# A decoder kernel's step table found anew, with a charge in its planner for changes between bf16 and fp32 operands on TensorE

## The chip, the cores and the metric

One core of one Trainium2 chip runs the whole kernel. The time is device microseconds (us), the median of several runs. The engines are TensorE (PE; its weight loads are PEld), VectorE (DVE), ScalarE (ACT), GpSimd (POOL) and SyncE (SP), which only issues DMAs here.

## The reference, cut to what matters

Twelve sublayers follow each other on `x` of 4 batches x 256 tokens x 128 channels, all fp32:

```python
x = _layernorm(x + _L0_attn_ref(x, ...))         # state-space scan ("mamba")
x = _layernorm(x + _L0_xattn_ref(x, ctx, ctx))   # attention over a context
x = _layernorm(x + _L0_ffn_ref(x, ...))          # attention, then 8 experts, top 2, with a capacity
x = _layernorm(x + _L1_attn_ref(x, weight))      # attention whose values are 128 wide per head
x = _layernorm(x + _L1_xattn_ref(x, ctx, ...))
x = _layernorm(x + _L1_ffn_ref(x, ...))          # 8 experts
x = _layernorm(x + _L2_attn_ref(x, ...))         # causal attention
x = _layernorm(x + _L2_xattn_ref(x, ctx, mask))  # attention with a bias and a mask
x = _layernorm(x + _L2_ffn_ref(x, ...))          # 8 experts, tokens sent to slots
x = _layernorm(x + _L3_attn_ref(x, ...))         # linear attention
x = _layernorm(x + _L3_xattn_ref(x, ctx, ...))   # gathers the nearest context rows, then attention
x = _layernorm(x + _L3_ffn_ref(x, ...))          # 8 experts
```

Attention has 16 heads of 8 channels.

## The kernel before

The work is cut into 2378 steps, each a tuple such as `("P2", a, b, i)`: a kind, a sublayer's number, a batch and an index. A step uses one engine or several in turn: `SM` is scores on TensorE and then their row maximum on VectorE, `P2` is scores again, transposed and shifted by the maximum, on TensorE and then exp on ScalarE, `PV` is the weighted sum of values. `lanes()` puts the steps into 47 queues with a fixed order inside each (one for each batch's chain of sublayers, one for all `SM`, one for all `P2`, and so on). The string `ORDER` says from which queue the next step is taken, one letter for each step. This gives one list of all steps, and each engine's program is this list, cut to the steps that the engine has a part in, with semaphore waits for what a step reads. So `ORDER` alone sets what each engine does after what.

`plan()` goes through the list once, when the program is built, with the durations in `COST` and `cost()`, the time `HOP` that a result takes from one engine to the next, and `needs()`. It decides two more things: which of the eight PSUM banks a TensorE step gets (the bank that comes free first), and where TensorE gets `FILL` steps, matmuls on a free bank that nobody reads. They are put in where the planner sees TensorE idle for over 0.8 us (`FILL_OVER`), for 0.6 of the gap. No time of `plan()` is used on the chip in another way.

What a matmul of each kind looks like matters for the change. The scores of `SM` (L1087) and `P2` (L1116) are bf16 with contraction over 48 or 50 rows, and two heads run side by side in the two halves of the array's rows, on two banks. Before them a causal step has L1082 or L1106 and a masked `P2` has L1111: bf16 over all 128 rows. `MT` (L1096) is bf16 on 16 columns of the array. `MB` and `MC` (L1013) are bf16 over 96 rows. `PV` (L1129) is fp32 on 32 columns, with four heads side by side in the columns. Nearly all else is fp32 over 128 rows and 128 columns: `MA` (L1017), `XT` (L1027), `QK` (L1057), `ZV` (L1139), `Y` (L1155), the experts' `MH` (L1227) and `MO` (L1233). `FILL` (L1001) is bf16 over the whole array.

The times below call a place in the kernel by its line. `held` keeps which step had a bank before, and TensorE waits for the semaphore `read[kind]` of that step, by its count, before it writes there.

Of the kernel before, what the change touches and what calls it, by code (L numbers as in the profile page):

```python
# [54 lines left out]

COST = {
    "DT": ((PE, 1.8), (ACT, 0.7)), "BC": ((PE, 1.2), (DVE, 3.0)), "DZ": ((PE, 0.9), (ACT, 2.0)), "DL": ((ACT, 0.75), (DVE, 1.4)),
    "MX": ((ACT, 0.72),), "MB": ((PE, 0.24), (DVE, 2.34)), "MC": ((PE, 0.22), (ACT, 0.6)), "ME": ((POOL, 1.25),), "MN": ((PE, 0.05),), "MA": ((PE, 0.95),),
    "MY": ((DVE, 0.9), (PE, 0.4)),
    "STAT": ((DVE, 1.2), (POOL, 0.95)), "XB": ((POOL, 0.8),), "STAT2": ((DVE, 1.95), (POOL, 0.95)), "NORM": ((DVE, 0.62),), "XT": ((PE, 0.22), (ACT, 0.33)),  # L60
    "GQ": ((PE, 0.43), (ACT, 0.3)), "GS": ((PE, 0.43), (DVE, 1.7)), "GT": ((PE, 0.44), (ACT, 0.5)), "GM": ((PE, 0.86), (ACT, 0.3)),
# [18 lines left out]
KB = {"RH": 256, "RL": 512, "ROWS": 768, "SHIFT": 8, "GB": 8, "GL": 256, "BL": 192, "YS": 192, "LW": 1024,  # L80
      ("LD", "w"): 2048, ("LD", "part"): 2048, ("LD", "wide"): 1024, ("LD", "mask"): 1536, ("LD", "mask2"): 512, ("LD", "mask3"): 512, ("LD", "lin"): 2048,
      ("LD", "select"): 576, ("LD", "ctx"): 128, ("LD", "zero"): 1920}
HOP = 0.15
PIPE = 0.2
FILL, FILL_OVER, FILL_ONE = 0.6, 0.8, 0.22
TABLE = {"P2": "exp", "LF": "exp", "DZ": "exp", "MX": "exp", "DL": "exp"}
# [127 lines left out]
def needs(st, feats):  # L214
# [248 lines left out]

SYMBOLS = "abcdefghijklmnopqrstuvwxyzABCDEFGHIJKLMNOPQRSTU"
ORDER = (
    "aaaaaaaababaccdebcbaeddacedbcaebaceddbabcebdaceaebcbddacedabcedbacebdcaedbcaebaecbdcaebdcaeddbacedaecebadecdcnbbonacebda"
    "baednecdcaebacbeddonlblacokabocbeedadcedcamblbedaecbadaleccdemmmggggemdepqpmggfphggpglfgfsklhgqhiiggijimhfqmgijmgiqgvihg"
    "ilgggjjnnhlhmgniiknfnniijgghnglmggmmitjghliigggijghghjigioimohiggjugoioiojgoiggmhojiglghghjhgplpiiikggpgjiphpgpijiipukmm"
    "ihgljggjimmqqlghghifqgigqmjqkiiSfggfiqjhgmqiiglgfhsjjmgghivtninilgnggjihnighngimnjgjnighminwggwwwwjinghhngiookggiojiorrr"
    "ggijiiirojxxoghxhxgjowpggpowywyxihxhyiypoikyoiyxxjjipiiyyyyiprjnpnpjpwwwwqqpwwxxrrrxqpynnxxwwyyyrnwqqwlkxxxwxryyrqlrmmmx"  # L470
    "xqwyqxwxywwyyyxqoyqrrrwyyywwoooyyxggxoyggwlwmygkyglhxwgpkxgkhwxxpkkkxwwxpggiyprkyimyijxjpmhxhyllggygykmgggyiyygmyjjjjqjq"
    "gmqkikkkkgiiqgjkjqhgghhlgjkjjmigjjghgRijjijjljnhijmmikjijhjjnijkgggjnkkgilggijjlggmmmjkhjjhggikkkgjjjihgokgikijjohijjjig"
    "ojgjiglmlmgjjRjjgijkjjgpkikkigkpkgmhhhhpgjijjgiggljgjijjkiglhmjimhjjgjjijjijijijiiqggiqjhmgikgqihggljgjhgimlnngigignjhmi"
    "nhhniggjiinmigjgnkinjgiiioonrhggjowgrgowwggxrokgwwhxwhwwigxgojyiyyxxihiyrjyoighixxhxyjyiipjypoyyipjnnniporiirwwwwpjjnwpw"
    "wxxxxprrxqlyqxpmwlykxqyqqypyqrrmxwxywyyyqwqwwrxxyymxwwwooroyxqwxyyyrxxxrwyogwgllgyrryggxyyywtpphwmmgwpwgxxxygygphwlxiyyy"
    "yxlmxigghgyymyhgmqkmiqigjjiqqiTghiglggslijhggggggjmhignmnihggnjninihgiinjnmgilggijglggjkhiihmmhkggojoimivhgoggooijiiuggi"
    "ojghghojlpigpgglkipisippgmpgjjhhiiiiimhpiggjmgjlqqihqggiggTijQgqtlhqmmiqgiggjiiggihqvimjigjlghhnlTkggnghmmiiggnigigjunjn"
    "gggiimgiinRihgjjonhohggghokiogRoiigihjhiggoignjiigiijoojkphhipzBBBpiiijiBiRjippiiCjACDjCwqqqDwwqqEwwFEwwpFDwEwpqFwEpCwRF"
    "GqwEwFwqEwEFDwwFECwwzEDwwGFFwBBBEwFEwwFEwwEwwBGFwFEECCFGFDADCwwGHwCEwwFEwwFEHHHnwwnFGDwEwooEFwnwIIwFEwIIDFEwwIIEIwFwEFJJ"
    "oCDwwJFJGEwwFJEKwwFEwGwJFEwwFwGKKKKKJUEEFFGIIHHLHLLLIJLMLLLIMLLLIHNNNNLNKKNJNLNJOMPRqOOLLLKOPpJJLpLNNNKNKIPLMKLqLNNINNLL"  # L480
    "JMIOOLJOOKILPPNNNNNNnKNJnnpnnnnnJLnILPLMKINnLKOOJJOOLLnKKMLLLnIMPINNNnJNPINNIMlJNOONKLOJKlPlLLLOMPKJlMLlLLoKILoLoMoINoNo"
    "oNJNNJqolUmloKINIooJoLLKkOOONNJoPKLLLIPlOINNNIPKNlMNJlOLOmmNNPgNJKLJOKMOLLLPpLLLlggNlppppINppppNKNNllJINNIpMJgkgOOPNJpLK"
    "OMLOUKKLLpggLLLpLPlgNPNNllNOghNgmmmhNNNgOgROOghlPhPqlgiilglqqqqqqqhqggUiqqmqgijmhgijqimlgiiljljhiikhnnglignlgnilngjjmgnl"
    "hhgniinwmwwgingmgirrjwjghihioiowwoxrxkwgxygjryxiiooyggjgyiiyhoxgowgxyiwgjhggjoiwiwhpyhoxpijipwwxprrjiyiyiipppwxyyxjpjywr"
    "qqxxxxywypqyqqwwwrrqxwqxryyxyyxxxyqywywqrwrrxxxwoowxxnnnrryywwxxoryyywwwyyywpypwpxxyyyyyxxxyyyyqqq"
)


# [5 lines left out]
def plan():  # L494

    queues = lanes()
    feats = [st[1:] for q in queues for st in q if st[0] == "LF"]
    heads = [0] * len(queues)
    free, done, listed = [0.0] * 5, {}, []
    until, place = [0.0] * 8, {}  # L500
    in_table, moved = None, 0.0
    for symbol in ORDER:
        j = SYMBOLS.index(symbol)
        st = queues[j][heads[j]]
        heads[j] += 1
# [24 lines left out]
        if st[0] == "MY" and st[1] % 2:  # L530
            until[place[("MN", st[1] // 2), 0]] = t + HOP
        if st[0] == "LR":
            until[place[("LN", *st[1:]), 0]] = t + HOP
        if st[0] == "STAT" and SUBLAYERS[st[1]] not in (("attn", SELF_WIDE), ("moe", DISPATCHED)):
            until[place[stat_source(st), 0]] = t + HOP
# [29 lines left out]
def decoder(nc, I, scratch, gate_rows_out, lin_out, slots_in, slots_out, out):  # L565
# [12 lines left out]
    with ExitStack() as ctx:  # L578
# [398 lines left out]
        def _(pe):  # L977
# [1170 lines left out]
```

## Time and profile before

| | |
|---|---|
| median of 3 runs | 1210.09 us (1208.85 to 1210.41) |
| profiled execution: its own time | 1201.47 us |
| profiled execution: span, first to last instruction | 1199.6 us |
| mean granted TensorE clock | 0.976 of full |
| TensorE busy | 1106.6 us (92%) |
| VectorE busy | 911.0 us (76%) |
| ScalarE busy | 700.7 us (58%) |
| GpSimd busy | 332.1 us (28%) |
| DMA | 93.01 MB, 78 GB/s in the mean |

An engine's busy time is a sum over the span. The end of a matmul is modelled, so that successive matmuls overlap in the records: the time from the start of one to the start of the next is the better measure of what one costs.

### The profile page before, as it was taken

What the parts mean: (1) busy time and instruction counts of PE and PEld (TensorE: products, weight loads), DVE (VectorE), ACT (ScalarE), POOL (GpSimd) and SP (SyncE); (2) the same over time, 40 slices, a digit from 0 to 9 for tenths busy, and PEclk for the clock granted to TensorE, in tenths of its full rate; (3) what the DMA queues carried; (4) which work ended last, traced back from release to release, by engine and by line L of the source; (5) the groups of instructions that cost most, each with busy time, mean ns of one, the idle gap of its engine ahead of it and who ended that gap; (6) DMA issues with size and microseconds to landing.
All of it is one profiled execution on the core that took longest, in us unless ns stands there. A gap on an engine that the chain in (4) does not pass through costs nothing. (4 is left out here: it accounts for less than half of the span.)

```text
span 1199.6 us, 24688 instructions
## 1 busy us (share of the span) xinstructions
PE 1106.6 (92%) x8142; PEld 699.3 (58%) x8153; DVE 911.0 (76%) x2363; ACT 700.7 (58%) x1532; POOL 332.1 (28%) x443
## 2 busy tenths in 40 slices
PE   7878988899999999999998999988989999999997
PEld 2233545458667775677554454654657676765576
DVE  6999697778788889657788872427798999876654
ACT  4443678775545458775565545436575665558552
POOL 4546223002211111011223323030474454421001
PEclk9988699899999999999999999999999999999999
DMA  7003224222323222033524414120100010132012
GB/s 243 1 0 106 80 86 164 65 72 73 105 63 103 82 86 66 33 94 119 147 81 164 156 72 161 52 70 25 44 19 2 1 34 26 58 121 86 16 52 70
DMA packets 75787, 93.01 MB, mean 78 GB/s; under 512 B 6537, under 2 KB 60273, under 8 KB 73841
## 3 DMA queue, kind: packets, MB, share of 16 engines
q1 hardware_dynamic: 74640, 89.34, 23.3%
q0 software_dynamic: 1024, 2.10, 0.6%
q8 instruction: 70, 1.15, 0.4%
q14 instruction: 53, 0.43, 0.1%
HBM read 64.25 MB, written 28.67 MB: 77 GB/s over the span
## 5 line engine op out<-in xcount | busy, mean ns | idle before, releaser
L1420 ACT ACTIVATE P<-bank 128x512 f32<-128x512 f32 (+1 forms) x448 | 230.6, 585 | 92.8 <-PE bank L1116 91.3
L1832 DVE TENSOR_REDUCE mx<-bank 128x2 f32<-128x512 f32 x320 | 200.7, 683 | 24.7 <-PE bank L1087 22.9
L1633 POOL TENSOR_SCALAR rstd<-mv 128x2 f32<-128x2 f32 x56 | 15.0, 268 | 414.0 <-DVE mv L1684 335.2
L1129 PE MATMUL bank<-P,V 128*32 128x256 f32 (+1 forms) x1536 | 101.0, 386 | 3.1 <-ACT P L1420 1.9
L1233 PE MATMUL bank<-room 128*128 128x256 f32 x384 | 97.2, 389 | 2.1 <-DVE room L1980 2.1
L1227 PE MATMUL bank<-xT,room 128*128 128x256 f32 x384 | 95.6, 387 | 0.0
L1087 PE MATMUL bank<-QKR 48*128 48x256 bf16 (+1 forms) x896 | 82.8, 276 | 11.4 <-DMA QKR<-split_rows 7.2
L1116 PE MATMUL bank<-QKR 50*128 50x256 bf16 (+1 forms) x896 | 85.0, 274 | 5.5 <-DMA QKR<-msT 2.1
L1233 PEld LDWEIGHTS bank<-room 128*128 128x128 f32 x384 | 69.8, 191 | 18.2 <-issue 6.0
L1980 DVE TENSOR_TENSOR room<-room 128x512 f32<-128x512 f32 x96 | 63.4, 700 | 21.8 <-DMA room<-gate_rows 21.1
L1227 PEld LDWEIGHTS bank<-xT,room 128*128 128x128 f32 x384 | 69.4, 190 | 13.7 <-issue 5.6
L1643 POOL TENSOR_TENSOR qk<-qk,parts 128x256 f32<-128x256 f32 x56 | 38.6, 710 | 136.1 <-ACT parts L1389 136.1
L1464 ACT ACTIVATE room<-bank,b 128x256 f32<-128x256 f32 x128 | 52.7, 478 | 26.7 <-PE bank L1227 26.2
L1139 PE MATMUL bank<-room,P 128*128 128x129 f32 x512 | 66.4, 281 | 0.1
L1129 PEld LDWEIGHTS bank<-P,V 128*32 128x32 f32 x1536 | 42.6, 111 | 39.5 <-issue 15.7
L1139 PEld LDWEIGHTS bank<-room,P 128*128 128x128 f32 x512 | 60.4, 191 | 8.3 <-issue 7.0
L1087 PEld LDWEIGHTS bank<-QKR 48*128 48x128 bf16 x896 | 32.1, 95 | 55.9 <-issue 36.4
L1116 PEld LDWEIGHTS bank<-QKR 50*128 50x128 bf16 x896 | 31.0, 95 | 57.2 <-issue 37.0
L1987 DVE TENSOR_TENSOR room<-bank,room 128x512 f32<-128x512 f32 x30 | 20.7, 689 | 53.2 <-PE bank L1207 42.2
L1207 PE MATMUL bank<-room 128*128 x120 | 58.6, 596 | 0.0
L1431 ACT COPY og<-bank 128x256 f32<-128x256 f32 x96 | 36.3, 380 | 38.0 <-PE bank L1129 37.3
L1727 DVE TENSOR_TENSOR_SCAN room<-room 128x512 f32<-128x512 f32 x32 | 55.5, 1734 | 1.1
(288 smaller groups left out, 2421.7 us busy)
## 6 DMA issues: line engine op xcount, KB each, us to landing
QKR<-split_rows SPq DMA_DIRECT2D x112, 192.0 KB
room<-gate_rows SPq DMA_DIRECT2D x48, 256.0 KB, 3.6
split_rows<-parts SPq DMA_DIRECT2D x56, 192.0 KB, 2.4
split_rows<-parts SPq DMA_DIRECT2D x56, 128.0 KB, 2.0
room<-in_w SPq DMA_DIRECT2D x6, 1024.0 KB
room<-in_w SPq DMA_DIRECT2D x3, 2048.0 KB
split_rows<-parts SPq DMA_DIRECT2D x56, 64.0 KB, 1.7
room<-in_mask SPq DMA_DIRECT2D x4, 512.0 KB, 7.9
```

Of the source, the lines that this page charges most:

```text
L1087: last = nc.tensor.matmul(psum(st, p)[:, t * S:t * S + nk], QKR[rows, buf, 0, i, t * 128:(t + 1) * 128], QKR[rows, buf, 1, i, 0:nk], start ...
L1116: last = nc.tensor.matmul(psum(st, p)[:, t * S:t * S + S - q0], QKR[rows, buf, 1, i, t * 128:(t + 1) * 128], QKR[rows, buf, 0, i, q0:S], s ...
L1129: last = nc.tensor.matmul(bk[32 * j:32 * j + 32, q0:S], V[:, n % 2, t, 4 * g + j, :], P[:, (e - 1 + j) % NBUF_P, t * S:t * S + S - q0], st ...
L1139: last = nc.tensor.matmul(bk[:, q * S:q * S + D + 1], P[:, (e - 1) % NBUF_P, t * S + q * 128:t * S + (q + 1) * 128], Z[:, b % 2, t, h, 0:D ...
L1207: last = nc.tensor.matmul(bk[:, :], x, w[:, bass.DynSlice(expert[j] * 512, 512)], start=True, stop=True)
L1227: last = nc.tensor.matmul(bk[:, j * S:(j + 1) * S], w1s[m][:, e, j * 128:(j + 1) * 128], xT[:, S * b:S * (b + 1)], start=True, stop=True)
L1233: last = nc.tensor.matmul(y[:, 0:S], w2s[m][:, e, j, :], hT[:, slot_of(b, e), j * S:(j + 1) * S], start=(m == 0 and (e, j) == (0, 0)), sto ...
L1420: nc.scalar.activation(P[:, (e - 1) % NBUF_P, 0:width], psum(st, p)[:, 0:width], ACT.Exp, scale=SCALE).then_inc(read[k], 1)
L1464: last = nc.scalar.activation(to[:, j * S:(j + 1) * S], bk[:, j * S:(j + 1) * S], ACT.Gelu if m == 1 else ACT.Relu, bias=b1[:, m // 2, e, ...
L1727: V_.tensor_tensor_scan(hs[:, (i - 1) % 2, :], abar[:, (i - 1) % 2, :], bu[:, (i - 1) % 2, :], 0.0, ALU.mult, ALU.add).then_inc(scan_done, 1)
L1832: V_.reduce_max(to, sc[:, :].rearrange("p (t s) -> p t s", t=TPB), AX.X).then_inc(read[k], 1)
L1980: V_.tensor_tensor(to, to, gb[:, e:e + 1, :].to_broadcast([128, 2, S]), ALU.mult).then_inc(scaled, 1)
```

## The change

Three things are edited. The durations of the planner: `HOP` from 0.15 to 0.2 us, `MB` on VectorE from 2.34 to 2.48, `GB` and `BI` on TensorE, the `STAT` of the sublayer whose tokens are sent to slots from 2.0 to 2.7, two of the `GATE` steps. The planner: TensorE is charged 0.09 us when it goes from a step with fp32 operands to one of `SM`, `P2`, `MT`, `MB`, `MC` (bf16), and 0.04 us on the way back. The table `ORDER` is another one, with the same 2378 letters in another order. The kinds, the number and the instructions of the steps are the same.

The fourth edit is bookkeeping: for a bank that a `STAT` step empties, the count that TensorE waits for is now that of the `STAT` steps in the list, and not that of the steps that filled the bank.

```diff
-    "MX": ((ACT, 0.72),), "MB": ((PE, 0.24), (DVE, 2.34)), ...
+    "MX": ((ACT, 0.72),), "MB": ((PE, 0.24), (DVE, 2.48)), ...
-    "RANK": ((PE, 0.45), (DVE, 0.6)), "GB": ((PE, 0.42), (ACT, 0.3), (SP, 0.35)), ...
+    "RANK": ((PE, 0.45), (DVE, 0.6)), "GB": ((PE, 0.5), (ACT, 0.35), (SP, 0.35)), ...
-    "BI": ((PE, 0.4),), ...
+    "BI": ((PE, 0.6),), ...
-HOP = 0.15
+HOP = 0.2
+NARROW = ("SM", "P2", "MT", "MB", "MC")
+TO_NARROW, TO_WIDE = 0.09, 0.04
...
-        return ((DVE, 2.0 if SUBLAYERS[st[1]] == ("moe", DISPATCHED) else ...
+        return ((DVE, 2.7 if SUBLAYERS[st[1]] == ("moe", DISPATCHED) else ...
...
-        return ((PE, 0.4), (DVE, (3.3, 3.1, 2.2, 2.5)[st[1]]))
+        return ((PE, 0.4), (DVE, (3.3, 3.1, 2.3, 3.2)[st[1]]))
...
 ORDER = (
-    "aaaaaaaababaccdebcbaeddacedbcaebaceddbabcebdaceaebcbddacedabcedbacebdcaedbcaebaecbdcaebdcaeddbacedaecebadecdcnbbonacebda"
...
+    "aaaaaaaababaccbbedaecbdacebdacebdadceaceddbbaecacedbabecbdaecdaceddbacedbacedbbacebaecbddacedabecaecdebacdedbaecdnbbonac"
...
@@ plan()
+            if eng == PE and narrow != (st[0] in NARROW):
+                t += TO_WIDE if narrow else TO_NARROW
+                narrow = not narrow
...
-        if st[0] == "YC":
-            until[place[("BI", *st[1:]), 0]] = t + HOP
...
+        if released_by(st):
+            until[place[released_by(st), 0]] = t + HOP
...
+def released_by(st):
+
+    if st[0] == "YC":
+        return ("BI", *st[1:])
+    if st[0] == "MY" and st[1] % 2:
+        return ("MN", st[1] // 2)
+    if st[0] == "LR":
+        return ("LN", *st[1:])
+    if st[0] == "STAT" and SUBLAYERS[st[1]] not in (("attn", SELF_WIDE), ("moe", DISPATCHED)):
+        return stat_source(st)
+    return None
...
@@ decoder()
+    emptied, emptyings = {}, {}
     for st in steps:
+        if st[0] == "STAT" and released_by(st):
+            emptied[released_by(st)] = emptyings[released_by(st)[0]] = emptyings.get(released_by(st)[0], 0) + 1
...
-            eng.wait_ge(read[st[0]], banks_of(st) * count[st])
+            eng.wait_ge(read[st[0]], emptied.get(st, banks_of(st) * count[st]))
...
-                            pe.wait_ge(read[old[0]], banks_of(old) * (count[old] - 1) + nth + 1)
+                            pe.wait_ge(read[old[0]], emptied.get(old, banks_of(old) * (count[old] - 1) + nth + 1))
```

The two tables can be read out letter by letter through the queues, which gives counts of the order alone. "Run" means steps that follow each other on TensorE.

| read out of the table | before | changed |
|---|---|---|
| steps | 2378 | 2378 |
| changes between bf16 and fp32 steps on TensorE | 572 | 434 |
| changes of the shape in which the array is used (rows 32, 64 or 128; columns 32, 64 or 128) | 832 | 737 |
| of these, entries into a fp32 step over the whole array | 266 | 211 |
| runs of `SM` and `P2` | 261 | 201 |
| steps of such runs from the third of a run on | 68 | 108 |
| TensorE steps with at most one other between them and the TensorE step that feeds them (also by way of other engines) | 87 | 57 |
| TensorE steps that keep their order with each other | | 1020 of 1674 |

By sublayer, the 95 fewer changes of shape are: wide-value attention 35, the gathered attention 24, the second attention 11, linear attention 11, the second expert layer 9, the masked attention 7, the transposes of `x` 6, others within 2 either way, and the causal attention 8 more. Between `MA` and `MB` or `MC` there are 53 changes before and 50 changed.

## Rows read from the trace of the kernel before

**Rows 1.** The page, busy us by engine, then TensorE's clock in 40 slices

```profile
PE 1106.6 (92%) x8142; PEld 699.3 (58%) x8153; DVE 911.0 (76%) x2363; ACT 700.7 (58%) x1532; POOL 332.1 (28%) x443
...
PEclk9988699899999999999999999999999999999999
```

**Rows 2.** Windows: length, then busy us (instructions) by engine, clock, DMA share, GB/s

```profile
40.00:80.00 40.00, 30.27 (x88) 11.03 (x87) 37.93 (x39) 17.24 (x29) 18.51 (x17) 0.91 0.00 1
...
280.00:760.00 480.00, 464.06 (x3684) 293.17 (x3694) 362.83 (x1259) 279.94 (x630) 98.76 (x153) 1.00 0.32 103
880.00:1170.00 290.00, 277.98 (x2134) 195.47 (x2133) 236.91 (x472) 176.93 (x405) 96.51 (x125) 0.99 0.13 42
```

**Rows 3.** Timeline of TensorE in the wide-value attention: start us, length us, what

```profile
401.13 2.05 PE L1139 MATMUL bank<-room,P 128*128 128x129 f32 x16
...
403.44 2.95 PE L1139 MATMUL bank<-room,P 128*128 128x129 f32 x24
...
406.64 0.44 PE L1027 MATMUL bank<-ident,x_tok 128*128 128x128 f32 x2
406.91 1.06 PE L1139 MATMUL bank<-room,P 128*128 128x129 f32 x8
407.90 0.39 PE L1087 MATMUL bank<-QKR 48*128 48x256 bf16 x4
408.23 1.16 PE L1139 MATMUL bank<-room,P 128*128 128x129 f32 x8
409.32 0.39 PE L1116 MATMUL bank<-QKR 50*128 50x256 bf16 x4
409.55 0.38 PE L1087 MATMUL bank<-QKR 48*128 48x256 bf16 x4
```

**Rows 4.** Timeline of TensorE in the state-space scan

```profile
97.55 1.02 PE L1017 MATMUL bank<-room,ident 128*128 128x512 f32 x2
98.41 0.59 PE L1001 MATMUL bank<-identb 128*128 128x512 bf16 x2
98.84 0.38 PE L1013 MATMUL bank<-QKR,pick 96*128 96x512 bf16 x1
99.06 1.07 PE L1017 MATMUL bank<-room,ident 128*128 128x512 f32 x2
99.97 0.38 PE L1013 MATMUL bank<-QKR,pick 96*128 96x512 bf16 x1
```

**Rows 5.** Timeline of TensorE in the causal attention

```profile
602.11 0.38 PE L1082 MATMUL bank<-causal_q,identb 128*128 128x256 bf16 x2
602.43 0.34 PE L1087 MATMUL bank<-QKR 48*128 48x128 bf16 x4
```

**Rows 6.** Waits of TensorE's score matmuls: us in total, times, longest

```profile
PE bank L1087 <- DMA QKR<-split_rows: 7.2, 4, 2.7
...
PE bank L1116 <- ACT P L1420: 1.5, 2, 0.9
PE bank L1116 <- DVE mx L1832: 1.2, 4, 0.5
PE bank L1087 <- ACT P L1420: 1.2, 3, 0.6
...
PE bank L1087 <- DVE mx L1832: 0.9, 2, 0.7
```

**Rows 7.** Timeline: the maximum of one `SM` and the exp of one `P2`

```profile
400.77 1.26 DVE L1832 TENSOR_REDUCE mx<-bank 128x2 f32<-128x512 f32 x2
...
401.40 1.09 ACT L1420 ACTIVATE P<-bank 128x512 f32<-128x512 f32 x2
```

**Rows 8.** Windows around the longest stretch at a low TensorE clock

```profile
105.00:115.00 10.00, 6.17 (x28) 2.30 (x27) 8.95 (x16) 1.78 (x4) 5.72 (x6) 0.83 0.26 76
115.00:140.00 25.00, 24.21 (x156) 14.28 (x154) 15.29 (x40) 12.71 (x30) 5.86 (x10) 0.52 0.25 81
```

**Rows 9.** Groups of instructions: the `FILL` matmuls

```profile
L1001 PE MATMUL bank<-identb 128*128 128x512 bf16 x127 | 35.6, 394 | 0.0
```

More of the change, by code:

```diff
@@ L57 @@
     "DT": ((PE, 1.8), (ACT, 0.7)), "BC": ((PE, 1.2), (DVE, 3.0)), "DZ": ((PE, 0.9), (ACT, 2.0)), "DL": ((ACT, 0.75), (DVE, 1.4)),
-    "MX": ((ACT, 0.72),), "MB": ((PE, 0.24), (DVE, 2.34)), "MC": ((PE, 0.22), (ACT, 0.6)), "ME": ((POOL, 1.25),), "MN": ((PE, 0.05),), "MA": ((PE, 0.95),),
+    "MX": ((ACT, 0.72),), "MB": ((PE, 0.24), (DVE, 2.48)), "MC": ((PE, 0.22), (ACT, 0.6)), "ME": ((POOL, 1.25),), "MN": ((PE, 0.05),), "MA": ((PE, 0.95),),
     "MY": ((DVE, 0.9), (PE, 0.4)),
@@ L66 @@
     "OT": ((PE, 0.43), (DVE, 0.48)), "OX": ((PE, 0.27), (ACT, 0.33)), "Y": ((PE, 0.54),),
-    "RANK": ((PE, 0.45), (DVE, 0.6)), "GB": ((PE, 0.42), (ACT, 0.3), (SP, 0.35)), "GL": ((SP, 0.47),),
+    "RANK": ((PE, 0.45), (DVE, 0.6)), "GB": ((PE, 0.5), (ACT, 0.35), (SP, 0.35)), "GL": ((SP, 0.47),),
     "MH": ((PE, 0.86), (ACT, 0.6)), "HG": ((DVE, 0.6),),
-    "BI": ((PE, 0.4),), "MO": ((PE, 0.87),), "YC": ((ACT, 0.33),), "YT": ((PE, 0.22),),
+    "BI": ((PE, 0.6),), "MO": ((PE, 0.87),), "YC": ((ACT, 0.33),), "YT": ((PE, 0.22),),
     "SLOT": ((PE, 0.6), (DVE, 2.2)), "EID": ((PE, 1.0),), "SC": ((POOL, 2.6),), "BL": ((SP, 0.5),), "BT": ((PE, 0.35), (ACT, 0.42)),
@@ L97, in cost @@
     if st[0] == "STAT":
-        return ((DVE, 2.0 if SUBLAYERS[st[1]] == ("moe", DISPATCHED) else 1.55 if st[1] in RMS_SUBLAYERS else 1.2), (POOL, 0.95))
+        return ((DVE, 2.7 if SUBLAYERS[st[1]] == ("moe", DISPATCHED) else 1.55 if st[1] in RMS_SUBLAYERS else 1.2), (POOL, 0.95))
     if st[0] == "SM" and st[1] == MASKED:
@@ L465 @@
 ORDER = (
-    "aaaaaaaababaccdebcbaeddacedbcaebaceddbabcebdaceaebcbddacedabcedbacebdcaedbcaebaecbdcaebdcaeddbacedaecebadecdcnbbonacebda"
-    "baednecdcaebacbeddonlblacokabocbeedadcedcamblbedaecbadaleccdemmmggggemdepqpmggfphggpglfgfsklhgqhiiggijimhfqmgijmgiqgvihg"
-    "ilgggjjnnhlhmgniiknfnniijgghnglmggmmitjghliigggijghghjigioimohiggjugoioiojgoiggmhojiglghghjhgplpiiikggpgjiphpgpijiipukmm"
-    "ihgljggjimmqqlghghifqgigqmjqkiiSfggfiqjhgmqiiglgfhsjjmgghivtninilgnggjihnighngimnjgjnighminwggwwwwjinghhngiookggiojiorrr"
@@ L470 @@
[L470 to L485, printed above, removed]
+    "aaaaaaaababaccbbedaecbdacebdacebdadceaceddbbaecacedbabecbdaecdaceddbacedbacedbbacebaecbddacedabecaecdebacdedbaecdnbbonac"
@@ new lines @@
+    "nabcbeedacebnddaeaccbeddolabkloccabboeedadeccadebmmmdlbkatealccggdgegdeepqpqpggffphgglmmmhgflmsfggghiiqggiqgSjihggijihlg"
+    "ijigmmlgfhfmjhgiihmnngigmnjinnggijiingnghihglggkjgljughmiiooghigojigooghijoiigmmkoghilvggjjmglhiihmppgipgigjppggitjiipgi"
+    "jghpsmjlhgmflgqqkgghifqgigiiqjugqghhqgijimmkqfhiggvgiljjhgligmnhingigngjininmhhigngjjigknigniimjwwwwghgghwnwggwgnworigog"
+    "rjikgogijxhihoioiyjyxygxojoxrxhiipporypwwxyppxiiopjhyyypoiixpryyrjjniniwwwnpjwxwnqqywqpyrrxxxrnqylqlwyyqkqxyxxxxryyyywqo"
@@ new lines @@
+    "wwwrywkwomxxkoqmryxxwmyqoggyoyxxxrwlglxgmggyywywggggyywwwpkpxhmywykkkwrrrkxxxxpxpymhgggxhypiyhyggiyjgihlyyyggmiljjqkqkmm"
+    "jjjjjgiikkqiijjkqjkgqhgggklljjjjjghminkgkiginjmjgihhjjjgijjmnkigjiRglggjhkjjjggligjjkmkkgigjjkgghkkgmkmhkoghihoijkjgijjo"
+    "jjhigjjiggillmmjjjjggijjjkjkpkhigpkkighjmjiigjjhjhgipjgiglljjjjgiijjjjgiijmhjqghijiiqigjgqgijimRmlgggjhmhihlgnTinkgiigjn"
+    "gghinnnjiiimkjgghmnijniiigwjQoknhhrgorrwwggggwwwxwxrowgigjyohoigoyixxjxgioyyjgohxihixhpyyiipjypjoiiiypxryyijpwrrrpjnpnww"
@@ new lines @@
+    "qnqwpxxwwxxxxnwxsqwpyqllyxyyyyyqrrkwqyyyxqwroyorqmmowwxwwxxwmwyyqoyryllmmwxxxxxrwyyyryyggppwwxwwrgxgggxxpwywyhmggghypyyx"
+    "lgmgglyxxyhggiyyuggyiihigqqqjjmmhhiiiigggqjlmkjhhilinnmmigiggnjnngjiiinktnigghlggggljjhggmioomigshhggogiiohoggmjghjoiiio"
+    "ggkighlggjmhjligippiggijhgpjppikiiiipmgjpgjhgmlqgqiihlgivggiggmiqjggjqghTqiigiimggmhqhijgiuqjlnnkkhnlgmggitighgiigjnnjgg"
+    "igTginiiimmghhhijjooRnggggonoiiiiogogjhRjiggiigiiovhhhjojkizBBBpphBiiiiAjjiRCiiijDCpjwCqqpDqpwwqpEqpwwFEwqwFEwwDqEpwwFFw"
@@ new lines @@
+    "ECqwEDFwGwFEwCwFEwwGzEDwFwFEwwFEwRwGFBBBEBCwwFEwwFwEEFFDAwwGGHHHCwDCEwwFEHwwFEnwwFDnwEonwEFwowIGFECIwwIEFIwwCIIEDFIGwwJE"
+    "JFDwwJFEwwGJJFEwwJKFEwwFEwJwGFwoKKKKKKEEFFGHIMMHIHLLLILLJLLLMJIMLLINNNNNNNNJJLLKKROOLLLLLLOpKJKOILPLLIpHPPNNNNNKNNLJOONJ"
+    "LqIOOLIPMMpPKNKLLLLnNNJqnnnJnNqnnUMKnINnLLIIMNNPInNKJOOOLnLPJOKNNNNLnnJJLIOPlNNNKONLKKJlLOlOLIMKlPPoMLJLLLIolNooNINNooLo"
+    "NJKJlooNlIMLIkPKoNmOOKoNLmLmLLOJLoJIPoOMKNINNJNlMIPMNNNONOUKJKLJlOLlOLPPLLLKLpglLgglINlppmKNpNpJpMlmINpppNNINMJNpJKpKLgp"
@@ L486 @@
+    "OgLOOOKLLLLphgLkLhlPgggPglPlNUNNNNNNmNRlggOOOOgPPlqgUiilqqlgqqqqqqghigqmqqhijhgimjqighliigmlljjhiiknnlggnlnnihglgjiinggg"
+    "nmljhinwhiimjwgnjiggiwookwohiwmorrwwowxrrxxhggoijyjggiyygigoyixghhowgiwwjjxxgixiygppoyhiipywwpjphjiwxrxxiiiyywppyywjrrxx"
+    "xxrpjynqqxyypynqywqxyrrrrnwwwwqqqyyxqyyxxwwywowqyyrxxyyowwwwxxyyxowwxxrrrxxxxxyyywpppyxyyyyyyyyqqq"
 )
@@ L500, in plan @@
     until, place = [0.0] * 8, {}
-    in_table, moved = None, 0.0
+    in_table, moved, narrow = None, 0.0, False
     for symbol in ORDER:
@@ L527, in plan @@
             until[at] = 1e9 if st[0] in HELD_FOR else t + HOP
-        if st[0] == "YC":
-            until[place[("BI", *st[1:]), 0]] = t + HOP
[L530 to L535, printed above, removed]
+        if released_by(st):
+            until[place[released_by(st), 0]] = t + HOP
         done[st] = t + LANDING.get(st[0], HOP)
```

## Prediction

> **What bounds the kernel now.** I read the page first, for the share of each engine, then windows by stage, then the timeline of TensorE, to see what one step costs beside the next, and last its waits. TensorE is busy 1106.6 of 1199.6 us, 92% [rows 1]. That is an average over different limits, so I cut the span. From 280 to 760 us TensorE is busy 464.06 of 480 us, from 880 to 1170 us 277.98 of 290 us, and no other engine passes 82% in either [rows 2]: there TensorE is the bound, for 770 of 1200 us, and it is idle for only 15.9 + 12.0 = 27.9 us in them. In the state-space scan it is different: from 40 to 80 us VectorE is busy 37.93 of 40 us and TensorE 30.27 [rows 2]. Time that TensorE no longer needs is gained in the two long stretches, and mostly not in the scan. So the question is what the new order takes off TensorE.
>
> **What a change of step costs on TensorE.** The busy sum hides it, since modelled ends overlap the next start. Starts show it.
> - In the wide-value attention, 24 matmuls of L1139 last 2.95 us and 16 last 2.05 [rows 3], so each adds 0.1125 us and eight take 0.90. From the start of eight (406.91) to the next line's start (407.90) are 0.99 us: going from the whole array to the scores, which use it in two halves of rows, costs 0.09 us.
> - From scores to scores (L1116 at 409.32, L1087 at 409.55) are 0.23 us. From scores to L1139 (407.90 to 408.23) are 0.33 us: 0.10 more to go back.
> - Eight of L1139 last 1.06 us behind L1027, which is fp32 over the whole array too, and 1.16 us behind scores [rows 3]; and their next line starts 1.09 us after them instead of 0.99. A fp32 step over the whole array, entered from another shape, so loses a further 0.10 us inside.
>
> A trip to the scores and back costs 0.29 us, and the planner now charges 0.13 for it. Is it the type or the shape? In the scan fp32 and bf16 alternate, both over the whole array (96 rows count as that). Two bf16 matmuls of L1001 take 0.43 us start to start, 0.215 each, and one of L1013 with fp32 behind it (98.84 to 99.06) takes 0.22: nothing for the change. The way back, two of L1017, is 0.86 us in one place and 0.91 in another, so 0.05 at most [rows 4]. In the causal attention two bf16 matmuls of half that width (0.107 each, 0.21) are followed by bf16 scores after 0.32 us (602.11 to 602.43) [rows 5]: 0.10 us, with the type unchanged. So the shape costs, and the charge meets it only because scores differ in both.
>
> [...]
>
> **The change part by part.**
> - Fewer changes of shape. The table has 832 before and 737 after, 95 fewer, at 0.10 us each: 9.5 us. Entries into a fp32 step over the whole array fall from 266 to 211, 55 fewer at another 0.10 us: 5.5 us. Together 15.0 us of TensorE. I didn't time `PV`'s column split from rows and give it the same price. If only the type counted, at the planner's own charge, 138 fewer changes at 0.065 each would be 9.0 us. The lower bound is 0 (all hidden by other waits), the upper 15.0. By sublayer at least 80 of the 95 lie in sublayers that run mainly in the two stretches where TensorE is 96% busy [rows 2]; I take 0.9 of it: **-13.5 us**.
> - Longer runs of scores. Steps from the third of a run on go from 68 to 108, 40 more. Each holds two of eight banks until ScalarE (1.09 us for a `P2`) or VectorE (1.26 us for an `SM`) has emptied them [rows 7], while TensorE could issue one each 0.23 us. Bounds of the price: 0 where other banks are free, and 1.09 - 0.23 = 0.86 us where each waits, which is 34 us for 40. Before, all waits of score matmuls for these two engines are 1.5 + 1.2 + 1.2 + 0.9 = 4.8 us [rows 6], 0.07 us for each of the 68. I take that, since it is of the same kind of step: **+3 us**.
> - Looser dependencies. TensorE steps with at most one other step between them and their producer go from 87 to 57. Such a step comes too early if the engine between needs longer than that one step. Bounds: 0, and 30/87 of TensorE's whole idle time of 93.0 us [rows 1], 32 us. In the two stretches it is idle 27.9 us, and 30/87 of that is 9.6. I take a third, since most waits have another cause: **-3 us**.
> - Durations of the planner. They move no instruction themselves. They set which bank a step gets and where `FILL` goes. `MB` at 2.48 is nearer to the chip than 2.34: VectorE is 95% busy in the scan [rows 2], so what it does there sets the pace, and it isn't less work. `FILL` has 127 matmuls [rows 9] at 0.215 us, 27 us, nearly all in the first stages, where TensorE waits anyway. A fifth more or fewer in a wrong place would be 5 us either way; I take 0.
> - The clock. [...] I see no reason for a side and take 0.
> - The bookkeeping of `STAT`. In both tables the `STAT` steps come in the order of the steps that they read, kind by kind, so each wait has the number that it had: 0.
> - SP and GpSimd. 193 of SP's 238 steps and 212 of GpSimd's 248 keep their order, with a median shift of one place or none. TensorE's score matmuls wait for the rows by DMA 7.2 us in 4 places [rows 6]; that could go or double, so bounds of -7 and +7, and since the DMAs keep their order I take 0.
>
> Sum: -13.5 + 3 - 3 = -13.5 us. The profiled execution took 1201.5 us (its span 1199.6 and 1.9 around it) and would take 1188.0. The median of the runs is 8.6 us above it, and I carry that over: 1210.1 - 13.5 = **1196.6 us**, 1.1% less.
>
> **The rivals.**
> - Hidden. The TensorE time that goes is given back to ScalarE, VectorE and the DMAs, since a cluster of steps only shifts where it waits. For it: VectorE is busy 76 and 82% of the two long stretches [rows 2], and fuller in places. Against it: 27.9 idle us in 770 leave little to hide in. Time: 1207.7 to 1212.5.
> - Longer runs make it slower. One mechanism: the third and later steps of a run find no bank. At 0.86 us for each of the 40 more, this is 1210.1 - 16.5 + 34.4 = 1228. It meets the time of before at 16.5/40 = 0.41 us each, and is slower by 0.2% from 0.47 us. Against it: before, it was 0.07 us [rows 6]. For it: runs of 6, 7 and 9 steps need 12 or more bank places, and before there was one run of 6 and none longer.
> [...]
> - The charge is at the wrong place, so that the order gives up slack for changes that cost nothing. Between `MA` and `MB`/`MC` the number of changes moves from 53 to 50, so this could only cost in the scan, within 2 us: 1199.
>
> **How the numbers follow.** A measurement of this kernel tells no change from 0.2%, 2.4 us. The forecast with its own spread (1189 to 1204, the charge's rival in it) gets 0.62. Partly hidden (1204 to 1207.7) gets 0.09, the clock's gain (under 1189) 0.10: faster is 0.81. Within 0.2%, by hiding or by a new low stretch, 0.08. Slower, by longer runs or by a low stretch and partial hiding together, 0.11. Cut at both ends, the range that leaves out 2 in 10 is 1186 to 1211.
>
> **What would show it right or wrong.** In the profile after: score steps in pairs more often, the same 0.09 to 0.10 us at each change of shape, and TensorE's busy sum lower by a few us in the stretch of the wide-value attention. A gain that lies instead in the first 150 us (the clock or the scan) would make the sum wrong even with the time right. The waits of L1087 and L1116 for `P` and `mx` should stay under 10 us; above 20 the second rival has it. Wrong too, if TensorE's idle time outside the scan grows by what the changes saved.

## The result, and the profile after

The changed kernel takes 1169.74 us (1167.10 to 1172.14, 4 runs) beside 1210.25 for the kernel before, ratio 0.9662 (0.9635 to 0.9689): 3.4% less, or 40.5 us. Forecast were 13.5 us less and a range down to 1186. Measured again beside the experiments, the ratio was 0.9659 (0.9625 to 0.9693).

The page of the changed kernel, busy us by engine and TensorE's clock in 40 slices:

```profile
span 1168.1 us, 24695 instructions
...
PE 1091.1 (93%) x8144; PEld 704.2 (60%) x8153; DVE 909.0 (78%) x2363; ACT 700.4 (60%) x1532; POOL 333.0 (29%) x443
...
PEclk9988798999999999999999999999999999999899
```

Beside [rows 1] the span is 31.5 us shorter, and it falls into two nearly equal halves: TensorE is busy 15.5 us less (1106.6 to 1091.1), and idle 16.0 us less (1199.6 - 1106.6 = 93.0 before, 1168.1 - 1091.1 = 77.0 after). The other engines do what they did.

The missing 9 of the 40.5 us are not in the traces: the profiled execution before took 1201.5 us, 8.8 less than the median of its runs, and that of the changed kernel took 1169.9, its median. The mean granted clock of the runs goes with it. The profiled execution before had 0.976; none of the 65 later runs of that kernel is above 0.975, and their median is 0.970 or 0.971 on every chip. The ten runs of the changed kernel have 0.977 to 0.983, with a median of 0.980. Among runs of the kernel before on one chip, one whose clock is 0.001 higher is 1.0 us shorter (65 runs, uncertain by 0.15). By an estimate from these numbers the changed kernel's higher clock goes with some 9 us of the gain in the medians, and with 1 us between the two traces.

The time also depends on the chip: the medians of the kernel before, beside the experiments, are 1200.7, 1200.5 and 1200.1 us in three sets, 1210.1 and 1207.7 in two. The changed kernel was timed only where the one before stood at 1210, so whether its ratio is the same on the others is not shown.

The timeline of TensorE in the wide-value attention of the changed kernel (L1102 and L1131 are the scores, L1154 is `ZV`):

```profile
392.78 0.39 PE L1102 MATMUL bank<-QKR 48*128 48x256 bf16 x4
393.00 0.38 PE L1131 MATMUL bank<-QKR 50*128 50x256 bf16 x4
393.32 2.05 PE L1154 MATMUL bank<-room,P 128*128 128x129 f32 x16
395.21 0.38 PE L1042 MATMUL bank<-ident,x_tok 128*128 128x128 f32 x2
395.43 1.95 PE L1154 MATMUL bank<-room,P 128*128 128x129 f32 x16
```

Scores now come in pairs, 0.22 us apart, and share one way in and one way out. The step costs are those of [rows 3]: 0.32 us from scores to `ZV`, and 2.05 us for its 16 matmuls behind scores where they take 1.95 behind a fp32 step of the same shape.

Waits of the score matmuls, to be read beside [rows 6]:

```profile
PE bank L1102 <- DMA QKR<-split_rows: 8.8, 9, 2.3
...
PE bank L1131 <- DVE mx L1847: 2.1, 4, 0.9
...
PE bank L1102 <- DVE mx L1847: 1.3, 4, 0.5
...
PE bank L1102 <- ACT P L1435: 1.2, 3, 0.6
```

They add up to 4.6 us for `P` and `mx`, where they were 4.8. The 40 more steps in long runs added no such wait.

**Where the time went, from the starts of the matmuls.** For each two matmuls that follow each other in a trace I took the time between their starts over the usual spacing of that kind. At a change of shape up to 0.098 us of it counts as shape; 0.095 to 0.125 us inside a fp32 step over the whole array counts as entry; what is left above 0.02 us is called waits. Of that column 14 to 27 us, by kernel, lie in stretches at the lower level of the clock, and `FILL` matmuls are not in it. Every clock record in these traces is at 1.00 or at 0.50 of full (0.50 from 125 to 135 us in the trace before, 1.00 from 145 to 200), and 0.50 is the lower level. The times are in us, with the changes that the trace shows (some matmul records are missing). "Clock" is the mean granted clock of the traced execution, and "planner" the time at which the changed planner sees the last engine done, for this table:

```
kernel                        changes  shape  entry  waits  median ratio  clock  planner
before                            827   78.7   23.0  164.6  1           0.976   1159.5
changed                           731   69.4   19.2  146.4  0.966       0.977   1124.0
new_table_old_planner             732   69.5   17.2  140.7  0.969       0.980   1124.0
old_table_fewer_shapes            725   69.0   18.6  178.7  1.006       0.972   1178.0
new_table_more_shapes             831   79.0   20.5  143.1  0.992       0.978   1162.5
new_table_moved                   735   69.8   17.2  150.3  0.991       0.976   1167.0
searched_old_model                876   83.1   24.8  136.6  0.981       0.983   1138.8
searched_old_model_2              849   80.6   22.6  145.6  0.979       0.980   1134.6
searched_new_no_charge            867   82.4   21.8  129.5  0.979       0.987   1131.0
searched_old_model_charge         754   71.6   20.4  135.8  0.972       0.985   1125.5
searched_old_model_charge_2       728   69.2   18.5  144.3  0.966       0.981   1125.2
searched_new_model                758   72.0   18.6  148.3  0.981       0.975   1118.8
searched_new_model_2              744   70.7   17.7  135.7  0.961       0.986   1120.0
searched_shape_charge             616   58.6   14.1  167.2  0.976       0.976   1136.5
searched_shape_calibrated         620   59.0   17.2  166.6  0.980       0.971   1132.0
```

From before to changed: shape -9.3, entry -3.8, waits -18.2, together -31.3 of the 31.5 us. So 13.1 us are the shapes and 18.2 are waits, for any engine or at the lower clock; both traces have nearly the same clock, so little of the difference is the clock's.

Does it lie in one stage? Windows from one sublayer's last normalisation to the next (a write of `x_tok`) show the busy time in the scan with the first attention, the second attention, the stretch that holds the wide-value attention, that from the second expert layer to the masked attention, and the linear attention. Before:

```profile
0.00:203.50 203.50, 166.39 (x1064) 79.23 (x1067) 171.39 (x284) 115.76 (x240) 83.53 (x106) 0.91 0.29 93
203.50:290.10 86.60, 79.54 (x677) 51.96 (x670) 63.42 (x206) 61.14 (x128) 12.99 (x24) 0.96 0.22 75
290.10:581.00 290.90, 284.96 (x2114) 198.12 (x2114) 232.33 (x702) 177.03 (x388) 47.70 (x81) 1.00 0.27 85
581.00:753.90 172.90, 162.90 (x1487) 82.05 (x1495) 119.78 (x523) 94.68 (x225) 47.26 (x66) 1.00 0.41 135
...
904.00:1075.80 171.80, 167.73 (x1271) 121.89 (x1274) 152.30 (x255) 101.15 (x223) 74.03 (x92) 1.00 0.12 39
```

Changed:

```profile
0.00:202.70 202.70, 165.48 (x1066) 79.16 (x1066) 171.16 (x282) 116.31 (x240) 84.02 (x108) 0.91 0.31 94
202.70:278.10 75.40, 71.73 (x658) 47.97 (x651) 60.19 (x202) 59.11 (x123) 10.56 (x18) 1.00 0.24 76
278.10:569.10 291.00, 283.70 (x2155) 203.88 (x2154) 236.50 (x714) 181.52 (x396) 51.62 (x83) 1.00 0.32 101
569.10:731.10 162.00, 155.97 (x1444) 79.19 (x1453) 117.54 (x514) 91.81 (x219) 47.24 (x66) 1.00 0.32 107
...
899.50:1047.30 147.80, 146.99 (x1137) 109.43 (x1135) 136.09 (x236) 86.01 (x194) 65.69 (x85) 1.00 0.14 45
```

The first 203 us are the same to a microsecond, clock included (0.91 in both): the scan gave nothing, and between these two traces neither did the clock there. From there TensorE's idle time falls in three of the four windows, 7.1 to 3.7, 10.0 to 6.0, 4.1 to 0.8 us, and rises from 5.9 to 7.3 in the one with the wide-value attention. In the first of the three the granted clock rises too, from 0.96 to 1.00. There the busy time, of which the prediction expected a few us less, falls by 1.3 us, with 41 more matmul records. A part of the work has moved over the borders (x1271 matmuls and x1137 in the last pair), so the lengths don't compare stage by stage. At equal amounts of matmul work done the gain grows evenly: 4 us after 165 us, 8 after 296, 12 after 530, 17 after 718, 24 after 937, 31 at the end. It is many small things and no single wait.

### The profile page after: what moved, and what is told of

The parts are those of the page before. It is cut to its first block and busy times, and to the rows that moved or that the text cites. A ratio compares the mean times of both kernels' runs of the same rounds, so it can differ in the third digit from the quotient of the medians.

```text
span 1168.1 us, 24695 instructions
## 1 busy us (share of the span) xinstructions
PE 1091.1 (93%) x8144; PEld 704.2 (60%) x8153; DVE 909.0 (78%) x2363; ACT 700.4 (60%) x1532; POOL 333.0 (29%) x443
## 5 line engine op out<-in xcount | busy, mean ns | idle before, releaser
L1102 PE MATMUL bank<-QKR 48*128 48x256 bf16 (+1 forms) x896 | 81.5, 276 | 16.0 <-DMA QKR<-split_rows 8.8
L1131 PE MATMUL bank<-QKR 50*128 50x256 bf16 (+1 forms) x896 | 82.2, 274 | 3.9 <-DVE mx L1847 2.1
L1102 PEld LDWEIGHTS bank<-QKR 48*128 48x128 bf16 x896 | 33.5, 96 | 56.4 <-issue 33.4
L1154 PEld LDWEIGHTS bank<-room,P 128*128 128x128 f32 x512 | 60.0, 192 | 6.7 <-issue 4.0
L1154 PE MATMUL bank<-room,P 128*128 128x129 f32 x512 | 63.6, 278 | 0.4 <-DVE og L1869 0.2
L1131 PEld LDWEIGHTS bank<-QKR 50*128 50x128 bf16 x896 | 32.1, 95 | 49.1 <-issue 33.1
```

The source lines that it names most:

```text
L1102: last = nc.tensor.matmul(psum(st, p)[:, t * S:t * S + nk], QKR[rows, buf, 0, i, t * 128:(t + 1) * 128], QKR[rows, buf, 1, i, 0:nk], start ...
L1131: last = nc.tensor.matmul(psum(st, p)[:, t * S:t * S + S - q0], QKR[rows, buf, 1, i, t * 128:(t + 1) * 128], QKR[rows, buf, 0, i, q0:S], s ...
L1154: last = nc.tensor.matmul(bk[:, q * S:q * S + D + 1], P[:, (e - 1) % NBUF_P, t * S + q * 128:t * S + (q + 1) * 128], Z[:, b % 2, t, h, 0:D ...
```

## The experiments

The ratio is always to the kernel before, on the same chip. "Table" is `ORDER`. Expectations in us were set for a kernel before at 1210; where it stood at 1200, compare the ratio. The lines `(new table)`, `(old table)` and the like stand for the letters.

**Which part of the change: the table or the planner.** In the kernel before, the new table, so with the planner of before:

```diff
-ORDER = (old table)
+ORDER = (new table)
```

> The new table with the planner of before (its durations, HOP 0.15, no charge), so that only the order is new, and banks and FILL go by the old model. Theory A (the order itself gives the gain: fewer changes of shape and later use of results): 1170 us, within 4 of the changed kernel. Theory B (banks and FILL, placed by the truer model, give a good part): 1180 to 1200.

1163.3 us, 0.9687 (0.9663 to 0.9711). And the old table in the changed kernel:

```diff
-ORDER = (new table)
+ORDER = (old table)
```

> The old table with the new planner: only banks and FILL change. Theory A: 1210 us within 4. Theory B: 1180 to 1200.

1197.07 us, 0.9964 (0.9944 to 0.9983). By itself the table gives 3.1% and the planner 0.4% (0.2 to 0.6): nearly all of the gain is in the table, and where the planner puts banks and `FILL` matters little.

**Moving steps by hand.** Three tables were made from the two by moving some 240 to 260 steps a few places, within what each step reads:

```diff
-ORDER = (old table)
+ORDER = (old table, 261 steps moved, 108 fewer changes of shape)
```

> The old table and planner, with 261 of 2378 steps moved by at most 5 places, so that changes of shape fall from 832 to 724 and entries into fp32 over the whole array from 266 to 222, while the steps with at most one other behind their producer stay 87. By the price of 0.10 us for each (152 in all) TensorE is relieved of 15 us: 1195 us if the shape counts in full, 1202 if half is hidden. If what counted in the new table is only that results are used later, 1210.

1207.45 us, 1.0056 (1.0034 to 1.0077): a little slower. The shapes fell as they should, by 14.1 us in the trace, but the waits rose by 14.1, and the planner put in 146 `FILL` matmuls for 127.

The new table with 241 steps moved, 96 more changes of shape:

> The new table and planner, with 241 steps moved by at most 4 places, so that changes of shape rise from 737 to 833 and entries into fp32 over the whole array from 211 to 265, with 57 steps close behind their producer as before the moves. Shape theory: +15 us, 1185 us. If only the later use of results counts: 1170 us.

1190.14 us, 0.9922 (0.9897 to 0.9947), which is 0.026 above the changed kernel's ratio and seemed to be the shapes and more. The control, 242 steps moved with the changes kept, says otherwise:

> The control for new_table_more_shapes: the new table with 242 steps moved by at most 4 places and the counts kept (736 changes of shape, 213 entries, 57 steps close behind their producer). If the 31 us that new_table_more_shapes lost were 15 for its shapes and 15 for the disturbance, this one is at ratio 0.978 to 0.98. If the shapes were all of it, 0.966. If the moves were all of it, 0.99 and above: then a table's worth lies mainly in how well each step is placed, and not in the counts.

1187.74 us, 0.9906 (0.9877 to 0.9935), as slow with the shapes unchanged. In both the planner saw new gaps and filled them: L1016 has 190 `FILL` matmuls in new_table_moved and 167 in new_table_more_shapes, against 127, so 14 and 9 us at 0.215 us. Whether these lie in waits or push work back is not shown, since neither was run without them. So these three don't price the shape. In the new table 240 steps, moved by at most four places without regard to timing, cost 0.025 of the ratio, some 30 us, with the shapes or without. The planner would have said so before any run: by its own sum the moved tables take 38.5 and 43.0 us more than the new one, and old_table_fewer_shapes by the old planner 1137.1 us where the old table takes 1114.2.

**The price of the shape in place.** One small matmul ahead of each of the 96 `MH` steps, over half the rows or over all:

```diff
 elif k == "MH":
+    nc.tensor.matmul(bk[:, 0:2], identb[0:64, :], identb[0:64, 0:2], start=True, stop=True, ...)   # or identb[0:128]
```

> The changed kernel with one more matmul ahead of each of the 96 MH steps, bf16, 64 rows, 2 columns, into the step's own bank, which the step then overwrites. It puts two changes of shape around it and one entry into a fp32 step over the whole array: 96 x (0.10 + 0.10 + 0.10) = 29 us of TensorE and some 4 us for the matmuls. Shape theory: 26 to 33 us above the changed kernel, 22 or more above tiny_matmul_whole_array. [...]

> The control: the same 96 matmuls over 128 rows, so that the type changes twice 96 times and the shape never. If the type cost 0.09 and 0.04 us, as the planner charges: 12 us and more above the changed kernel. Shape theory: the matmuls alone, 3 to 8 us.

The half array gave 1187.36 us, 0.9797 (0.9764 to 0.9830), the whole array 1174.30 us, 0.9694 (0.9659 to 0.9728), the changed kernel beside them 1168.93. The timelines of TensorE, half array:

```profile
301.79 0.17 PE L1241 MATMUL bank<-identb 64*128 64x2 bf16 x1
301.89 1.13 PE L1243 MATMUL bank<-xT,room 128*128 128x256 f32 x4
302.86 0.38 PE L1072 MATMUL bank<-xT,room 128*128 128x256 f32 x1
```

and whole array:

```profile
302.07 0.17 PE L1241 MATMUL bank<-identb 128*128 128x2 bf16 x1
302.10 1.11 PE L1243 MATMUL bank<-xT,room 128*128 128x256 f32 x4
```

From the small matmul to the next start are 0.10 us after half rows and 0.03 after all rows. In the medians over the 96 places, what is added is 0.098 before, 0.104 to the step, 0.107 inside it for half rows, 0.31 us in all; and 0.003, 0.029 and 0.086 for all rows, 0.12 in all. So a change of shape costs 0.10 each way, and going to bf16 in the same shape 0.003.

The 0.086 inside isn't the type's either. A fp32 step loses the same behind a fp32 matmul of 16 columns, as here in the changed kernel (291.75 to 292.69 is 0.94 us, the four of the same size after it take 0.87):

```profile
291.52 0.37 PE L1181 MATMUL bank<-chosen,ones 128*128 128x16 f32 x2
291.75 1.11 PE L1248 MATMUL bank<-room 128*128 128x256 f32 x4
292.69 1.03 PE L1242 MATMUL bank<-xT,room 128*128 128x256 f32 x4
293.56 1.03 PE L1248 MATMUL bank<-room 128*128 128x256 f32 x4
```

At 174 such places in all traces, behind fp32 matmuls of 8 or 16 columns and in steps whose own have 256 or 512, the median is 0.083; in such steps behind a bf16 matmul of 512 columns, where TensorE had not waited, it is 0.001 (125 places). So the type costs nothing, which the planner charges with 0.13 a trip.

The total grew by 18.4 and 5.4 us. Not all 96 places are new on TensorE: 20 of the steps are entered from another shape in any case, so the half rows add 162 changes and 76 entries, some 24 us, and the whole rows some 9. Of the 24 us three quarters arrive at the end (18.4, uncertain by 4), of the 9 about half (5.4, uncertain by 4); the difference is 13 us for 15.

**Without `FILL`.**

```diff
-FILL, FILL_OVER, FILL_ONE = 0.6, 0.8, 0.22
+FILL, FILL_OVER, FILL_ONE = 0.0, 0.8, 0.22
```

> The changed kernel without its FILL matmuls (127 of 0.215 us, 27 us of TensorE). If they only lie in gaps: the same time as the changed kernel within 3 us, with waits in their place. If they delay real work: faster by up to 10. If they hold the clock up: slower, with more time at the lower clock than the 55 us of the changed kernel's profile.

1177.56 us, 0.9729 (0.9695 to 0.9763), so 0.7% slower than changed_again, uncertain by 0.5%. The mean granted clock of its six runs is 0.959 to 0.973, with a median of 0.964, and that of changed_again's 0.979 to 0.983. The trace without `FILL` is of the fastest of them (1169.71 us, 0.973), which took as long as changed_again. The first 150 us, without and with `FILL`:

```profile
0.00:150.00 150.00, 102.93 (x486) 45.25 (x486) 127.29 (x178) 76.46 (x148) 68.14 (x82) 0.85 0.30 93
```

```profile
0.00:150.00 150.00, 118.92 (x584) 53.70 (x584) 128.07 (x178) 76.78 (x149) 68.99 (x82) 0.91 0.31 94
```

TensorE is busy 16 us less there, its granted clock is 0.85 instead of 0.91, and what `FILL` took comes back as waiting. So `FILL` lies mostly in gaps, and no run of the changed kernel without it has the clock of any with it.

> The changed kernel as it is, beside the three that follow, on their chip. The runs of the kernel before stood at 1210 us beside the first measurement and at 1200 beside all later ones, so the ratio and not the time carries over: 0.966 if it holds there too, 0.969 if it is that of the new table with the old planner.

This is the changed kernel beside the three; it gave 0.9659, as said above.

**Is it the charge, or any new search?** I searched tables of my own: from the old table, 8 million random moves of one to four steps, kept by the planner's sum under a falling threshold, the same for all but the seed. Each was run in the changed kernel, so with one planner for banks and `FILL`:

```diff
-ORDER = (new table)
+ORDER = (table found by the named model)
```

Without the charge:

> A table found by my own search (8 million random moves of steps from the old table, kept when the planner's sum falls, annealed), by the planner's model of before: HOP 0.15, no charge. Banks and FILL by the new planner, as in the three beside it. 883 changes of shape, 281 entries into fp32 over the whole array, 58 steps close behind their producer. If the search alone makes the gain (the old table was just not searched long enough), ratio 0.96 to 0.975 to before. If the charge is what makes it, 0.985 to 1.0: by counts the shape costs 6.6 us more than before, and the other waits fall.

> The search by the old model with another seed, to see how far two tables of one model lie apart. 857 changes of shape, 273 entries, 54 close steps. If the model sets the ratio: 0.981 within 0.003, that of the first seed. If tables of one model scatter by as much as the models differ: anywhere in 0.972 to 0.985.

> The same search with HOP 0.2 and the other new durations, without the charge. 873 changes, 282 entries, 46 close steps. Theory that the longer hand-over (later use of results) is what saves the waits: ratio 0.965 to 0.975. Charge theory: 0.98 to 0.99, some 5 us below the table of the old model.

1176.97 us, 0.9808 (0.9765 to 0.9852); 1181.92 us, 0.9786 (0.9759 to 0.9814); 1174.38 us, 0.9788 (0.9747 to 0.9830). With the charge on types:

> The same search, start and length with one thing added to the old model: the charge for changes between bf16 and fp32. 761 changes, 219 entries, 58 close steps. Charge theory: ratio 0.97 to 0.975, with some 20 us less than the table searched without it, of which the counts (122 + 62 fewer, at 0.10 us) are 18 us. Search theory: no difference between the two.

> The old model with the charge, another seed. 738 changes, 214 entries, 63 close steps. Charge theory: again near 0.972, and 0.01 below searched_old_model_2, of which the counts (119 and 59 fewer, at 0.10 us) are 18 us and something is given back in waits. Search theory: no difference from searched_old_model_2.

> My search, start and length as in the four before, by the whole new model (HOP 0.2, new durations, charge on types). 765 changes, 222 entries, 44 close steps. If charge and hand-over add up: 0.9716 for the charge alone, less some 0.002 for the hand-over as between the two tables without a charge, so 0.967 to 0.970, the changed kernel's own ratio.

> The whole new model, another seed. 752 changes, 217 entries, 53 close steps. If the first seed's 0.981 was an unlucky table: 0.970 to 0.974, as with the charge alone. If the model of the change has no merit over the old one: 0.975 to 0.985.

1165.19 us, 0.9716 (0.9672 to 0.9759); 1166.23 us, 0.9662 (0.9639 to 0.9686); 1177.18 us, 0.9811 (0.9757 to 0.9864); 1159.66 us, 0.9610 (0.9583 to 0.9638). The three without the charge mean 0.979, the four with it 0.970. So searching anew, by the very model of the old table, gives 2.0%, of which the planner for banks and `FILL` has 0.4% (old_table_new_planner), so some 1.7% for the order. The charge adds 0.9% in the mean, but the four scatter by 2% among themselves, with a standard error of 0.4% for their mean. It is likely and not settled. Under the old model both seeds have it, 0.9% and 1.2%. The changed kernel's 0.966 lies among the four.

More than half of the scatter goes with the clock: the runs of searched_new_model have a median of 0.974 of full, those of searched_new_model_2 0.986, and at 1.0 us for each 0.001 that is 12 us of the 17.5 between them. The other five tables have 0.979 to 0.983, with the charge or without, so what the charge gains isn't the clock's.

**The charge where the cost is.** On the shape instead of the type:

> The same search with the new durations and, in place of the charge on types, one on the shape as measured: 0.095 us for each change of shape and 0.105 us more on entry into a fp32 step over the whole array. 625 changes, 167 entries, 39 close steps. Shape theory: ratio 0.955 to 0.96, 8 to 16 us below the changed kernel. If the type is what costs, no better than the changed kernel (0.966).

> The search with the charge on the shape again, but with the TensorE durations of scores and sums of values freed from the change that they held in the mean (SM and P2 0.23, MT 0.12, PV 0.87, ZV 0.90, causal 0.50 us), so that a change isn't charged twice. 624 changes, 168 entries, 40 close steps. If double charging is what made searched_shape_charge wait (167 us of waits against 136): 0.955 to 0.962. If a table with so few changes waits in any case: 0.97 to 0.98.

1172.43 us, 0.9762 (0.9720 to 0.9804), and 1175.87 us, 0.9795 (0.9741 to 0.9848). The first missed its 0.955 to 0.96 by 1.6% and more; the second came out as its other case said, a table with so few changes waits in any case. They have the fewest changes of all, 616 and 620, and 12 to 19 us less of shape and entry than the tables with the charge on types; and 167 us of waits, 18 to 38 more than the other searched tables. Charging twice was not the cause, since the calibrated one waits as much. Two things go with it. Their runs have a low granted clock, with medians of 0.975 and 0.972, 4 to 10 us by the estimate above. And by the changed planner, whose charge on types both searches left out, they are 8 to 12 us worse than the changed table. A part of the waits is for the score rows by DMA. In searched_shape_charge:

```profile
PE bank L1102 <- DMA QKR<-split_rows: 10.5, 4, 4.9
...
PE bank L1097 <- DMA QKR<-split_rows: 5.6, 2, 4.3
```

A table searched with the charge on the shape and a hand-over of 0.3 us has no time on the chip, so whether later use of results cuts these waits is not known.

## Why the prediction was wrong

The direction was right, and the size was a third of what came. By its own steps:
- **What bounds the kernel** held. The gain in the traces lies after the first 203 us, and nothing came in the scan.
- **Fewer changes of shape, 15.0 us on TensorE, 13.5 taken.** The trace has 13.1 less, so the count and the local price were good. The share of it that reaches the end, taken as 0.9, is not refuted: the small matmuls over half the rows show three quarters, uncertain by 0.15, so some 10 us. The price is that of the shape and not of the type: with the small matmuls 0.098 and 0.104 us with a change of shape against 0.003 and 0.029 without. `PV`'s column split, which got the price without being timed, has it on the way in, 0.093 us from the whole array (L1129 in the trace before, 28 places). The part inside a fp32 step, counted as 55 entries at 0.10 us, measured 3.8 us and not 5.5: it comes behind short matmuls in the same shape too, and behind waits.
- **Longer runs of scores, +3 us**: 4.6 us of such waits for 4.8 before. The term was nothing, and the rival that made it 34 us is out.
- **Looser dependencies, -3 us**: this is the step that failed most. All waits fell by 18.2 us by the starts of the matmuls, and the idle time of the page by 16.0, where I had taken a third of a share of the two long stretches' idle time. A count of steps close behind their producer doesn't measure how well a table is timed: old_table_fewer_shapes kept 87 of them and waited 14 us more, and new_table_moved kept 57 and its ratio rose by 0.025. The tables searched without any charge waited 19 to 35 us less than the old one. The old table was far from the best that its own model finds (1114.2 us by the old planner's sum, where my searches by that model reach 1089.2 and 1088.1), and I had no term for that, although it was open before the result that a whole new table had been found. The planner's sum was at hand and not used: from the old table to the new it falls by 13.8 us by the old planner, and by 35.5, from 1159.5 to 1124.0, by the changed one.
- **Planner and bookkeeping, 0**: within 0.6%, and 0.4% by its median.
- **The clock, 0**: this failed too, in the medians. The two traces hide it: 0.91 in the first 203 us of both, the 25 us at 0.52 of [rows 8] broken up (0.72 from 115 to 140 us in the changed trace), other short stretches in their place, 55 us at the lower level in all for 59 before. But the trace before is of an execution with an unusually high clock, 0.976. No run shows the 0, or the gain by the clock that had a chance of 0.10. What the runs showed are medians of 0.970 and 0.980. By them, with 0.50 at the lower level, that level falls from some 72 us to 47, an estimate, and goes with some 9 us. That the clock is the cause of these 9 us rests on runs that differ by themselves; no experiment set it.
- **From the profiled execution to the median**: I carried 8.6 us over as if it stood still. It goes with that execution's clock, 0.976 beside a median of 0.970, and in the changed kernel, whose profiled execution took its median, there is no such gap.

With the range reaching down to 1186 the bounds of the terms were also not used: the looser dependencies had -9.6 and -32 us written beside them, and the range took in neither.

Settled: the table makes the gain, 13 us of it by fewer changes of shape on TensorE, 18 by waits spread over most of the kernel, the rest with a higher granted clock; and a new search by the old model brings about half of it. Open: how much is the charge and how much a lucky table, since two tables of one model differ by 2%; why one order has a higher clock than another; and why tables with the fewest changes of shape wait more. That `HOP` 0.2 alone does anything was not seen (0.979 with and without, both uncharged).

searched_new_model_2 has the lowest ratio, 0.961 (0.9583 to 0.9638), 0.5% below the changed kernel's. The intervals meet at their ends and the two were timed on different chips, so that it is the faster one is likely and not shown. Its page:

```profile
span 1155.8 us, 24677 instructions
...
PE 1082.0 (94%) x8133; PEld 697.0 (60%) x8144; DVE 908.3 (79%) x2363; ACT 703.4 (61%) x1535; POOL 332.5 (29%) x443
```

## What to carry to other kernels

When a change replaces a whole searched order, ask first how good the old one was by its own measure: fixing what the model misses may be worth less than the search that comes with it. Add up the planner's own sum for both orders before you add up terms: here it was nearer than the terms. Two orders that a model holds equal (1118.8 and 1120.0 us) can differ by 2% on the chip, so search several and time them. Moving steps by hand in a timed order for one cost alone gave back as waits all that it saved. Compare the clock of the profiled execution with that of the other runs before you carry a difference over.

## What the runs showed of the hardware

- A change between two shapes of TensorE's array cost 0.09 to 0.10 us: 0.098 us into half the rows at the 96 small matmuls of tiny_matmul_half_array (then 0.104 from the small matmul to the step, where it is 0.029 in tiny_matmul_whole_array), and 0.093 to 0.095 from the whole array to another shape in the median of each of the 19 kernels traced (223 to 349 places in each). Going from fp32 to bf16 in one shape added 0.003 us (tiny_matmul_whole_array, 96 places).
- The first matmul of a fp32 step over the whole array was followed 0.10 us late after a change of shape, where the step's matmuls have 129 to 512 columns (0.102 to 0.104 in the medians of 2218 places, all traces); with 128 columns the median is 0.055 (1807 places). In the same shape, in steps of 256 or 512 columns, it was so by 0.086 us after a bf16 matmul of 2 columns (tiny_matmul_whole_array), by 0.083 after fp32 ones of 8 or 16 columns (174 places, all traces), and by 0.10 behind fp32 ones after which TensorE waited over 0.3 us (39 places, all traces). So this part needed no change of shape.
- Matmuls that nobody reads, put in gaps, went with a granted clock of 0.91 instead of 0.85 in the first 150 us of the traces of changed_again and changed_no_fill, 0.980 instead of 0.964 in the medians of their runs, and 0.7% less time (1168.93 and 1177.56 us).
- Among runs of the kernel before on one chip, 0.001 more of granted clock over the run went with 1.0 us less of some 1205 (65 runs on five chips, 0.965 to 0.975).
